# Weighing the one-hot rows on ScalarE instead of VectorE in a graph layer kernel

## The chip, the cores and the metric

The kernel runs on one core of one Trainium2 chip. The metric is the device time of one launch in microseconds (us); lower is better.

## The reference, cut to what matters

The layer normalizes 6250 node rows of 160 features (a layer norm without weights, then relu), multiplies them by two sets of small matrices, and passes messages over 206,250 edges sorted by destination. The shape of the message step is all that matters here:

```python
h = relu(edge_attr_10 @ W_fc1 / sqrt(10)) * sqrt(2)
w = h @ W_fc2 / sqrt(100)                 # (E, 192) -> w0 (64), w1 (64), w2 (32), w3 (32)
y0, y1 = l0[edge_src], l1[edge_src]       # gathered node rows: 64, and 32 x 3
e0, e1 = edge_attr_4[:, :1], edge_attr_4[:, 1:4]
m0 = w0 * y0 * e0
m1 = (w1 * y0)[:, :, None] * e1[:, None, :]
m2 = (w2 * e0)[:, :, None] * y1
m3 = w3 * einsum('eud,ed->eu', y1, e1) / sqrt(3)
s0..s3 = segment_sum(m0..m3, edge_dst)    # per node, / sqrt(16)
out = x + self_part + 0.5 * (s0..s3 by the W_l2 matrices) / sqrt(96)
```

Every message is a product of edge weights and gathered rows, times one of the four attributes of its edge (or, for m3, with the attributes already in the dot product).

## The kernel before, in words

**Node stage (the first 67 us).** The node rows are loaded, normalized, multiplied and written to a table in DRAM. Rows for four edge groups (7, 12, 17 and 22) are computed apart and stay in SBUF (`ahead`), so those groups need no gather.

**Edge stage.** Edges come in tiles of 128 (one per partition) and groups of four tiles (T = 4): 403 groups. Groups go in turns of four (G = 4, slots `j` of the gathered rows `y`), turns in pairs of eight groups. Everything else is double-buffered by the parity `s` of the group. For each group g:

- GpSimd (`gather_group`, L427) issues four indirect DMAs, one a tile, that gather the rows of the sources into `y[:, j]`. It waits for `msg_done` of group g - 4, the last reader of that slot.
- TensorE computes the hidden layer (`fc1`, L976) into `ps_h`; ScalarE applies the relu (`relu`, L547); TensorE computes the 192 weights of each edge (`fc2`, L983) into `ps_w`.
- VectorE (`messages`) writes into slot 0 of `hot[:, s, t]` the one-hot rows: for each edge 32 columns, with a one at its destination's place in a window of 32 nodes (`which`, L746). It then multiplies the vectors of the gathered rows by three attributes (`edge_dots`, L722), writes slots 1 to 4 of `hot`, which are slot 0 times each of the four attributes (`weigh`, L752, one instruction over 128 x 512), sums the dots (`sum_dots`, L727), and forms the messages in three products (L733, L738, L743).
- TensorE (`windows`, L1028 and L1030) multiplies the messages with the weighed one-hot rows: a segment sum of the group into a window of 32 nodes, in `ps_s`. VectorE (`accumulate`, four adds, L815) adds that window to the sums `acc` in SBUF.

**The order of the work is written out by hand**, one instruction stream for each engine, with semaphores. TensorE's step g is `fc1(g)`, `fc2(g - 1)`, `windows(g - 2)`. VectorE's step g is `messages(g)`, `accumulate(g - 1)`. ScalarE's step g is `relu(g)` alone. From the fourth pair on, each pair of eight groups also finishes one block of 128 nodes: ScalarE normalizes it again (`normalize`, L496) at step 1, TensorE turns it (`turn_block`, L989 and L990) before `windows` of step 2, ScalarE copies the turned block (`move_block`, L552) at step 2 and the sums (`copy_block`, L556) at step 3; TensorE waits for that moved block (`hidt_done`) ahead of `fc1` of step 3, and multiplies (`last_linear`, L995 to L1001) at step 7; VectorE adds (`finish`, L800).

SyncE's queue loads the hidden inputs (L275), the indices (L282) and the attributes (L286) by half turns; the attributes wait for `msg_done` of the groups that read the slot before.

**The end.** After the last group's `fc2`, TensorE turns the last two blocks (each needs `normalize` from ScalarE, and both use `turn_block`), and only then runs `windows` of the last group but one, the blocks' own products (L1007, L1008), the sums' products of the last block but one (L1016 to L1018), the last group's windows (`last_windows`, L1040 and L1042), and the last block's products. VectorE's last steps are `last_messages` (the last group in two halves), and two times `accumulate` and `finish`.

Of the kernel before, what the change touches and what calls it, by code (L numbers as in the profile page):

```python
# [76 lines left out]
def gnn_layer(nc, x, x_a, src, dst, radial, attr, avec, w_lin, w_lin_z, w_self, w_self_z, w_last, wf1, wf2, out):  # L77
    ctx = ExitStack()
    with ctx:
# [116 lines left out]
        fc2_done = sem("fc2_done")  # L196
        hot_done = sem("hot_done")
        dots_done = sem("dots_done")
        dot_done = sem("dot_done")
# [58 lines left out]
        def _(sp):  # L258
# [11 lines left out]
            def load_half(i, c, first):  # L270
                k = i * 2 + c
                if not first:
                    sp.wait_ge(fc1_done, (k - 1) * HALF)
                    sp.sem_inc(sp_passed, 1)
                sp.dma_start(rad[:, c, :], radial[:, bass.ds(k * HALF * GE, HALF * GE)]).then_inc(ld_rad[c], 16)  # L275
                if not first:
                    for j in range(HALF * c, HALF * c + HALF):
                        landed = landed_of(i, j)
                        if not isinstance(landed, int) or landed > 0:
                            sp.wait_ge(gathered[j], landed * (16 * T))  # L280
                    sp.sem_inc(sp_passed, 1)
                sp.dma_start(idx[:, c, :], src[:, bass.ds(k * HALF * T, HALF * T)]).then_inc(ld_idx[c], 16)  # L282
                if not first:
                    sp.wait_ge(msg_done, (k - 1) * HALF * 4)
                    sp.sem_inc(sp_passed, 1)
                sp.dma_start(attr_sb[:, c, :, :], attr[:, bass.ds(k * HALF * T, HALF * T), :]).then_inc(ld_attr[c], 16)  # L286
# [87 lines left out]
        def _(pool):  # L374
# [44 lines left out]
            def gather_group(i, j, first, landed):  # L419
                if j % HALF == 0 or (isinstance(i, int) and i * G + j - 1 in AHEAD_GROUPS):  # L420
                    pool.wait_ge(ld_idx[j // HALF], i * 16 + 16)
                if not first:
                    pool.wait_ge(msg_done, (i * G + j - G + 1) * 4)
                    pool.sem_inc(pool_passed, 1)
# [48 lines left out]
        def _(act):  # L473
# [69 lines left out]
            def relu(g, s, first):  # L543
# [3 lines left out]
                nc.scalar.activation(hr[:, s, :], ps_h[0:N_RADIAL, s, 0:GE], ACT.Relu, scale=K_RADIAL).then_inc(relu_done, 1)  # L547

            def move_block(b, n, bank):

# [7 lines left out]
            def windowed():  # L558
                def pair(k, first, finish):
                    for j in range(2 * G):  # L560
                        relu(k * (2 * G) + j, j % 2, first and j < 2)
                        if finish and j == 1:
                            normalize(k - LAG, 0)
# [11 lines left out]
                for j in range(LEFT):  # L575
                    relu((TURNS - 1) * G + j, j % 2, False)
                for n, b in enumerate(range(IN_LOOP, BLOCKS)):
                    normalize(b, n)
# [26 lines left out]
        def _(dve):  # L605
# [143 lines left out]

            def weigh(g, j, s):  # L750
                dve.wait_ge(hot_done, g + 1)
                nc.vector.tensor_tensor(hot[:, s, :, 1:V, :], hot[:, s, :, 0:1, :].to_broadcast([P, T, 4, W]),  # L752
                                        attr_of(j, 0, 4).unsqueeze(3).to_broadcast([P, T, 4, W]), ALU.mult).then_inc(msg_done, 1)

            def messages(i, j):
# [9 lines left out]
                else:  # L765
                    rows = y[:, j, :, :]
                    dve.wait_ge(gathered[j], landed_of(i, j) * (16 * T) + 16 * T)
                    edge_dots(j, rows)
                weigh(g, j, s)
                dve.wait_ge(dots_done, g + 1)  # L770
# [7 lines left out]
            def last_messages():  # L778
# [4 lines left out]
                which(g, s)  # L783
                weigh(g, j, s)
                dve.wait_ge(fc2_done, g + 1)
# [120 lines left out]
        def _(pe):  # L906
# [113 lines left out]
            def windows(g, s, first, block=None):  # L1020

                pe.wait_ge(msg_done, g * 4 + 4)
                if not first:
# [9 lines left out]
            def last_windows():  # L1033

                g, s = EDGE_GROUPS - 1, (EDGE_GROUPS - 1) % 2
                pe.wait_ge(acc_done, (g - 1) * 4)
                for h in range(2):
                    pe.wait_ge(msg_done, g * 4 + 4 + 3 * h)
                    for t in range(h * (T // 2), (h + 1) * (T // 2)):
# [140 lines left out]
```

## Time and profile before

| What | Value |
| --- | --- |
| Time, median of 3 runs | 2081.51 us (2079.91 to 2085.27) |
| The profiled execution | 2082.13 us |
| its span | 2080.4 us |
| its mean granted clock of TensorE | 0.984 |
| TensorE busy (matmul) | 1961.0 us, 94% |
| VectorE busy | 1685.6 us, 81% |
| GpSimd busy | 1570.0 us, 75% |
| ScalarE busy | 352.4 us, 17% |

The times of the trace are microseconds from the start of the span; the span leaves out some 1.7 us of the execution's time. Busy shares are averages over the whole span. A row of the timeline gives the start, the duration, the engine, the line and what it writes and reads, and in brackets how long the engine had been idle and what released it. "x8" is eight instructions in one row. A matmul in fp32 leaves two records. A row of stretches gives the stretch, its length, the busy time of TensorE's matmuls and weight loads, VectorE, ScalarE and GpSimd with their counts, the granted clock, the share of the DMA engines and GB/s.

### The profile page before, as it was taken

The numbers are of one execution on the slowest core, as the hardware profiler recorded it, in microseconds if no ns is written. First come the engines' busy times: TensorE is split into PE (matmuls) and PEld (weight loads), VectorE is DVE, ScalarE is ACT, GpSimd is POOL, SyncE is SP. The second block draws the span as 40 slices with busy tenths as digits, with TensorE's granted clock in tenths as the row PEclk, the third lists the DMA queues.
The fourth block names the chain that finished last, engine by engine and source line by source line (L and its number), as shares of the span: only waits on it lengthen the run. The fifth ranks groups of instructions, "written<-read, shape, count | busy, mean of one in ns | idle before, by whom it ended". The sixth has DMA issues, their size and how long they took to land.

```text
span 2080.4 us, 42104 instructions
## 1 busy us (share of the span) xinstructions
PE 1961.0 (94%) x11562; PEld 1518.1 (73%) x11562; DVE 1685.6 (81%) x4682; ACT 352.4 (17%) x662; POOL 1570.0 (75%) x1639
## 2 busy tenths in 40 slices
PE   6999999999999999999999999999999999999998
PEld 6877777777777777777777777777777777777777
DVE  7799788888888888888888878888788888888887
ACT  6311111111111111111111111111111111111111
POOL 7877777777777777777777777777777777777775
PEclk9999999999999999999999989999999999999999
DMA  6322333333333333333333333333333323333322
GB/s 188 80 68 71 74 72 75 73 73 75 73 73 75 73 72 74 74 74 74 74 74 72 73 74 73 73 75 73 73 75 72 74 72 76 73 74 74 74 72 63
DMA packets 161200, 158.34 MB, mean 76 GB/s; under 512 B 88146, under 2 KB 133110, under 8 KB 161178
## 3 DMA queue, kind: packets, MB, share of 16 engines
q0 software_dynamic: 77376, 132.17, 25.8%
q1 hardware_dynamic: 82088, 24.49, 5.3%
q10 hardware_dynamic: 1714, 1.43, 0.2%
q8 instruction: 8, 0.13, 0.0%
q14 instruction: 14, 0.11, 0.0%
HBM read 149.92 MB, written 8.03 MB: 76 GB/s over the span
## 4 chain that ended last, share of the span: by engine, by line
POOL 36%; issue 26%; DMA 16%; DVE 14%; PE 7%; POOLq 1%; DVEq 0%; ACT 0%; ACTq 0%; SPq 0%
POOL y L427 36%; DMA y<-table,idx 15%; DVE hot L752 4%; DVE msg L733 4%; DVE dot L727 3%; PE ps_w L983 2%; PE ps_s L1028 1%; PE ps_h L976 1%; PE ps_s L1030 1%; DMA xres<-in_x 1%; DVE dots L722 1%; PE ps_w L938 0%; POOLq L438 0%; DVE acc L815 0%; DVEq L818 0%
## 5 line engine op out<-in xcount | busy, mean ns | idle before, releaser
L427 POOL DMA_INDIRECT y<-table,idx x1596 | 1520.6, 953 | 486.4 <-issue 444.8
L983 PEld LDWEIGHTS ps_w<-w_fc,hr 100*128 100x128 f32 x3224 | 516.3, 190 | 316.6 <-issue 316.6
L983 PE MATMUL ps_w<-w_fc,hr 100*128 100x192 f32 x3224 | 635.8, 341 | 0.0
L1028 PE MATMUL ps_s<-hot,msg 128*128 128x128 f32 x3216 | 458.0, 286 | 75.7 <-DVE msg L743 73.2
L547 ACT ACTIVATE hr<-ps_h 100x512 f32<-100x512 f32 x403 | 240.7, 597 | 1640.7 <-PE ps_h L976 1640.7
L1028 PEld LDWEIGHTS ps_s<-hot,msg 128*128 128x128 f32 x3216 | 404.5, 194 | 134.9 <-DVE msg L743 134.5
L722 DVE TENSOR_TENSOR dots<-y,attr_sb 128x384 f32<-128x384 f32 (+1 forms) x400 | 222.8, 557 | 284.9 <-DMA y<-table,idx 284.7
L976 PE MATMUL ps_h<-rad,w_fc 10*100 10x512 f32 x806 | 445.4, 632 | 0.2 <-issue 0.2
L1030 PE MATMUL ps_s<-hot,msg 128*128 128x128 f32 x3216 | 432.5, 278 | 0.0
L1030 PEld LDWEIGHTS ps_s<-hot,msg 128*128 128x128 f32 x3216 | 399.2, 195 | 0.0
L815 DVE TENSOR_TENSOR acc<-acc,ps_s 64x32 f32 (+1 forms) x1612 | 325.3, 202 | 44.5 <-PE ps_s L1030 4.1
L733 DVE TENSOR_TENSOR msg<-ps_w,y 128x512 f32<-128x512 f32 (+1 forms) x400 | 276.0, 690 | 17.4 <-PE ps_w L983 5.0
L752 DVE TENSOR_TENSOR hot<-hot,attr_sb 128x512 f32<-128x512 f32 x403 | 275.9, 685 | 0.0
L727 DVE TENSOR_REDUCE dot<-dots 128x128 f32<-128x384 f32 x404 | 236.2, 585 | 0.0
L738 DVE TENSOR_TENSOR msg<-ps_w,y 128x384 f32<-128x384 f32 (+1 forms) x400 | 218.5, 546 | 0.0
L976 PEld LDWEIGHTS ps_h<-rad,w_fc 10*100 10x100 f32 x806 | 100.2, 161 | 50.3 <-issue 3.1
L746 DVE TENSOR_TENSOR hot<-iota_w,dst_rel 128x128 f32<-128x128 f32 x403 | 117.9, 293 | 14.0 <-issue 1.1
L743 DVE TENSOR_TENSOR msg<-ps_w,dot 128x128 f32<-128x128 f32 x404 | 113.1, 280 | 0.0
L496 ACT ACTIVATE hid<-xres,shift,rstd 128x160 f32 (+1 forms) x98 | 47.9, 510 | 7.1 <-DVE shift L632 7.1
L995 PE MATMUL ps_s<-w_out,fin_in 128*128 128x160 f32 x94 | 25.4, 354 | 21.0 <-DVE msg L743 21.0
L995 PEld LDWEIGHTS ps_s<-w_out,fin_in 128*128 128x128 f32 x94 | 14.5, 191 | 33.2 <-issue 33.2
L556 ACT ACTIVATE fin_in<-acc 128x512 f32 (+1 forms) x49 | 30.5, 622 | 6.3 <-DVE acc L815 6.3
(95 smaller groups left out, 539.3 us busy)
## 6 DMA issues: line engine op xcount, KB each, us to landing
y<-table,idx POOLq DMA_INDIRECT x1596, 2.6
rad<-in_radial SPq DMA_DIRECT2D x202, 40.0 KB
xres<-in_x SPq DMA_DIRECT2D x7, 560.0 KB, 5.3
out<-xres SPq DMA_DIRECT2D x49, 80.0 KB, 1.6
table<-y SPq DMA_DIRECT2D x6, 560.0 KB, 3.7
idx<-in_src SPq DMA_DIRECT2D x202, 4.0 KB
attr_sb<-in_attr SPq DMA_DIRECT2D x202, 16.0 KB
dst_i<-in_dst ACTq DMA_DIRECT2D x1, 808.0 KB, 7.3
```

The costliest lines, as they stand in the source:

```text
L427: nc.gpsimd.indirect_dma_start(out=y[:, j, t, :], out_offset=None, in_=table, in_offset=bass.IndirectOffsetOnAxis(ap=idx[:, j // HALF, col ...
L547: nc.scalar.activation(hr[:, s, :], ps_h[0:N_RADIAL, s, 0:GE], ACT.Relu, scale=K_RADIAL).then_inc(relu_done, 1)
L722: nc.vector.tensor_tensor(dots[:, lo:hi, :, :], vectors(rows, lo, hi), attr_of(j, 1, 4, lo, hi).unsqueeze(3).to_broadcast([P, hi - lo, 3, ...
L727: nc.vector.tensor_reduce(dot[:, lo:hi, :], dots[:, lo:hi, :, :].rearrange("p t d u -> p t u d"), AX.X, ALU.add).then_inc(dot_done, 1)
L733: nc.vector.tensor_tensor(msg[:, s, lo:hi, 0:2 * MUL0].rearrange("p t (k u) -> p t k u", k=2), ps_w[:, s, lo:hi, 0:2 * MUL0].rearrange("p ...
L738: nc.vector.tensor_tensor(msg[:, s, lo:hi, 2 * MUL0:M - MUL1].rearrange("p t (d u) -> p t d u", d=3), ps_w[:, s, lo:hi, 2 * MUL0:NW - MUL1 ...
L752: nc.vector.tensor_tensor(hot[:, s, :, 1:V, :], hot[:, s, :, 0:1, :].to_broadcast([P, T, 4, W]), attr_of(j, 0, 4).unsqueeze(3).to_broadcas ...
L815: nc.vector.tensor_tensor(to, to, p[rows, cols].rearrange("p (v n) -> p v n", n=W), ALU.add).then_inc(acc_done, 1)
L976: nc.tensor.matmul(ps_h[0:N_RADIAL, j % 2, 0:GE], w_fc1[:, :], rad[:, j // HALF, (j % HALF) * GE:(j % HALF + 1) * GE], start=True, stop=Tr ...
L983: ins = nc.tensor.matmul(ps_w[:, s, t, 0:NW], hr[:, s, t * P:(t + 1) * P], w_fc2[:, :], start=True, stop=True)
L1028: nc.tensor.matmul(ps_s[:, s, 0:4 * W], msg[:, s, t, 0:P], hot[:, s, t, 1:V, :], start=(t == 0), stop=(t == T - 1))
L1030: ins = nc.tensor.matmul(ps_s[:, s, 4 * W:8 * W], msg[:, s, t, P:M], hot[:, s, t, 0:4, :], start=(t == 0), stop=(t == T - 1))
```

## The change

VectorE's `weigh` is taken out. ScalarE gets a `weigh` of its own: for each of four tiles and each of four attributes one activation (`Copy`, with the attribute of the partition's edge as its scale operand) over 32 columns, sixteen in a group. It follows `relu` of the next group in ScalarE's stream. A new semaphore, `weighed`, counts groups; `msg_done` counts three for each group instead of four. TensorE's `windows` waits for both, and so does SyncE's load of the attributes; GpSimd's gathers wait for `msg_done` alone.

```diff
@@ SyncE, load_half
                 if not first:
-                    sp.wait_ge(msg_done, (k - 1) * HALF * 4)
+                    sp.wait_ge(msg_done, (k - 1) * HALF * 3)
+                    sp.wait_ge(weighed, (k - 1) * HALF)
                     sp.sem_inc(sp_passed, 1)
@@ GpSimd, gather_group
-                    pool.wait_ge(msg_done, (i * G + j - G + 1) * 4)
+                    pool.wait_ge(msg_done, (i * G + j - G + 1) * 3)
@@ ScalarE
+            def weigh(g, j, s):
+
+                act.wait_ge(hot_done, g + 1)
+                for t in range(T):
+                    for k in range(4):
+                        ins = nc.scalar.activation(hot[:, s, t, 1 + k, :], hot[:, s, t, 0, :], ACT.Copy,
+                                                   scale=attr_sb[:, j // HALF, (j % HALF) * T + t, k:k + 1])
+                ins.then_inc(weighed, 1)
@@ ScalarE, windowed
                     for j in range(2 * G):
                         relu(k * (2 * G) + j, j % 2, first and j < 2)
+                        if j >= 1 or not first:
+                            weigh(k * (2 * G) + j - 1, (j - 1) % G, (j - 1) % 2)
                         if finish and j == 1:
                             normalize(k - LAG, 0)
...
                 for j in range(LEFT):
                     relu((TURNS - 1) * G + j, j % 2, False)
+                    weigh((TURNS - 1) * G + j - 1, (j - 1) % G, (j - 1) % 2)
+                weigh(EDGE_GROUPS - 1, LEFT - 1, (LEFT - 1) % 2)
                 for n, b in enumerate(range(IN_LOOP, BLOCKS)):
                     normalize(b, n)
                     move_block(b, n, n)
@@ VectorE
-            def weigh(g, j, s):
-                dve.wait_ge(hot_done, g + 1)
-                nc.vector.tensor_tensor(hot[:, s, :, 1:V, :], hot[:, s, :, 0:1, :].to_broadcast([P, T, 4, W]),
-                                        attr_of(j, 0, 4).unsqueeze(3).to_broadcast([P, T, 4, W]), ALU.mult).then_inc(msg_done, 1)
@@ VectorE, messages
                     edge_dots(j, rows)
-                weigh(g, j, s)
                 dve.wait_ge(dots_done, g + 1)
@@ VectorE, last_messages
                 which(g, s)
-                weigh(g, j, s)
                 dve.wait_ge(fc2_done, g + 1)
@@ TensorE, windows
-                pe.wait_ge(msg_done, g * 4 + 4)
+                pe.wait_ge(msg_done, g * 3 + 3)
+                pe.wait_ge(weighed, g + 1)
@@ TensorE, last_windows
                 pe.wait_ge(acc_done, (g - 1) * 4)
+                pe.wait_ge(weighed, g + 1)
                 for h in range(2):
-                    pe.wait_ge(msg_done, g * 4 + 4 + 3 * h)
+                    pe.wait_ge(msg_done, g * 3 + 3 + 3 * h)
```

## Rows read from the trace of the kernel before

**Rows 1.** Groups by line and shape: busy us, mean ns, idle before, releasers.
```profile
L427 POOL DMA_INDIRECT y<-table,idx x1596 | 1520.6, 953 | 486.4 <-issue 444.8 <-DVE msg L733 37.3 <-DMA idx<-in_src 2.7
...
L752 DVE TENSOR_TENSOR hot<-hot,attr_sb 128x512 f32<-128x512 f32 x403 | 275.9, 685 | 0.0
...
L547 ACT ACTIVATE hr<-ps_h 100x512 f32<-100x512 f32 x403 | 240.7, 597 | 1640.7 <-PE ps_h L976 1640.7
...
L722 DVE TENSOR_TENSOR dots<-y,attr_sb 128x384 f32<-128x384 f32 x398 | 222.1, 558 | 284.9 <-DMA y<-table,idx 284.7
```

**Rows 2.** Timeline in the middle of the edge stage, one group of VectorE.
```profile
1001.61 0.56 DVE L722 TENSOR_TENSOR dots<-y,attr_sb 128x384 f32<-128x384 f32 x1 [0.85 <-DMA y<-table,idx]
...
1002.08 0.68 DVE L752 TENSOR_TENSOR hot<-hot,attr_sb 128x512 f32<-128x512 f32 x1
...
1002.68 0.59 DVE L727 TENSOR_REDUCE dot<-dots 128x128 f32<-128x384 f32 x1
...
1005.17 0.94 POOL L427 DMA_INDIRECT y<-table,idx  x1 [0.30 <-issue]
...
1005.51 0.29 DVE L746 TENSOR_TENSOR hot<-iota_w,dst_rel 128x128 f32<-128x128 f32 x1
```

**Rows 3.** Timeline, TensorE alone, early in the edge stage: `fc1` of two groups running.
```profile
84.09 1.10 PE L976 MATMUL ps_h<-rad,w_fc 10*100 10x512 f32 x2
...
88.40 1.10 PE L976 MATMUL ps_h<-rad,w_fc 10*100 10x512 f32 x2
```

**Rows 4.** Timeline, ScalarE alone, node stage: activations back to back.
```profile
12.23 0.29 ACT L491 ACTIVATE std<-mean_var,eps 128x7 f32<-128x7 f32 x1
12.43 0.92 ACT L496 ACTIVATE hid<-xres,shift,rstd 128x160 f32 x2
```

**Rows 5.** Timeline at three gathers that took longer, each with VectorE's instruction ahead.
```profile
81.14 0.55 DVE L722 TENSOR_TENSOR dots<-y,attr_sb 128x384 f32<-128x384 f32 x1
81.22 1.29 POOL L427 DMA_INDIRECT y<-table,idx  x1 [0.30 <-issue]
...
98.17 0.29 DVE L746 TENSOR_TENSOR hot<-iota_w,dst_rel 128x128 f32<-128x128 f32 x1
...
98.29 1.00 POOL L427 DMA_INDIRECT y<-table,idx  x1 [0.30 <-issue]
...
2020.18 0.68 DVE L752 TENSOR_TENSOR hot<-hot,attr_sb 128x512 f32<-128x512 f32 x1
2020.34 1.35 POOL L427 DMA_INDIRECT y<-table,idx  x1 [0.30 <-issue]
```

**Rows 6.** Timeline of the end, from the last group but one on.
```profile
2064.74 0.56 DVE L722 TENSOR_TENSOR dots<-y,attr_sb 128x384 f32<-128x384 f32 x1 [0.83 <-DMA y<-table,idx]
...
2066.01 0.28 PE L989 MATMUL ps_h<-ident,hid 128*128 128x128 f32 x1
...
2066.44 0.38 ACT L552 ACTIVATE hid_t<-ps_h 128x256 f32<-128x256 f32 x1 [4.49 <-PE ps_h L990]
...
2066.72 0.51 ACT L496 ACTIVATE hid<-xres,shift,rstd 128x160 f32<-128x160 f32 x1
...
2067.08 0.94 POOL L427 DMA_INDIRECT y<-table,idx  x1 [0.30 <-issue]
2067.28 0.14 PEld L989 LDWEIGHTS ps_h<-ident,hid 128*128 128x128 f32 x1 [1.11 <-ACT hid L496]
...
2067.85 1.16 PE L1028 MATMUL ps_s<-hot,msg 128*128 128x128 f32 x8
...
2073.16 0.39 PE L1042 MATMUL ps_s<-hot,msg 128*128 128x128 f32 x2
...
2074.06 0.91 DVE L815 TENSOR_TENSOR acc<-acc,ps_s 64x32 f32 x4
```

**Rows 7.** TensorE at its lower clock: a timeline row, and a stretch of the end.
```profile
76.96 1.92 PE L1028 MATMUL ps_s<-hot,msg 128*128 128x128 f32 x8
...
2076.00:2078.00 2.00, 1.87 (x8) 1.46 (x7) 0.10 (x1) 0.00 (x0) 0.00 (x0) 0.50 0.00 0
```

More of the change, by code:

```diff
@@ L197, in gnn_layer @@
         hot_done = sem("hot_done")
+        weighed = sem("weighed")
         dots_done = sem("dots_done")
```

## The prediction

> **What bounds the kernel now.** I read the groups by line first. GpSimd's gathers are 1520.6 us busy and 486.4 us between one another [rows 1]: 2007 us of the span of 2080.4. The two parts add to 1.2575 us a gather, and what the group names as idle time is nearly all "issue", the fixed step between two gathers; the 37.3 us "<-DVE msg" are 122 waits of the same 0.3 us, so nothing was waited for. In the timeline GpSimd never pauses from its first gather to the last at 2067.08 [rows 6]. So the time is: a start of some 61 us, 1596 gathers, and a tail of 13 us. A group of four gathers takes 5.01 us.
>
> Next, how near the others are. VectorE is busy 81%, but each group it waits for the gathered rows: 284.9 us in 398 groups, 0.72 each [rows 1]. TensorE looks full at 94%, yet early on, while it works off a backlog, one `fc1` follows the other after 88.40 - 84.09 = 4.31 us [rows 3]. That is its own pace, 0.70 us under GpSimd's. ScalarE is nearly idle [rows 1]. An edit that relieves VectorE therefore gives nothing in the middle unless it reaches the gathers; what it may change is the gathers' length, the tail, and whether ScalarE becomes late.
>
> **Part 1, VectorE loses `weigh`.** 403 x 0.685 = 276 us of busy time go [rows 1]. In the timeline [rows 2] call D the start of the dots (1001.61): `weigh` starts at D + 0.47, the sum at D + 1.07, the next group's `which` at D + 3.90. Without `weigh` the sum must wait for the dots to be written: D + 0.56 and some 0.03, so it comes 0.48 earlier, and with it all that follows: `which` at D + 3.42. The next dots still wait for their gather. Worth in the middle: nothing; VectorE only idles 0.48 more in each group.
>
> **Part 2, the gathers get shorter in places.** A gather takes 0.95, but 35 of them took longer, by 9.0 us together; 26 lie before 211 us. Each had begun just behind a VectorE instruction with two inputs in SBUF: after `dots`, `which` or `weigh` [rows 5]. In all of them the same remainder fits: the gather is held until 0.43 us after `dots` began (81.22 - 81.14 + 1.29 - 0.95 = 0.42), 0.17 after `which` (98.29 - 98.17 + 0.05), 0.56 after `weigh` (0.16 + 0.40). On the gathers' chain every such hold is lost time. Early on VectorE is ahead or behind at TensorE's pace and meets the gathers at changing phases; those until 211 us cost 6.7. Afterwards, with only `dots` and `which`, a meeting at random costs (0.43^2 + 0.17^2)/2/1.25 = 0.085 us a group; 30 groups make 2.5. Gain 4.2 us. In the steady part I take nothing: a gather starts at D + 3.56 [rows 2] and `which` holds it until 3.42 + 0.17 = 3.59, a touch of 0 to 0.03 in some groups (the gap moves by 0.1 with the landing), while the 2.3 us of holds in the rest may shrink. Bounds: a gain of 9.0 (no holds left) and a loss of 6 (0.015 in 400 groups). I take a gain of 4.
>
> This agrees with the Trainium skill, SBUF — State Buffer, the reading of its port diagram: VectorE with two SBUF inputs and GpSimd reading SBUF lock one port pair against each other, ScalarE has its own. By that rule too, the moved work cannot hold a gather any more.
>
> **Part 3, sixteen activations.** The trace has none of 128x32 with one pointer operand. Nearest below: the 128x7 one with a pointer as bias, behind which the next starts 0.20 later (12.43 - 12.23); nearest above: 128x160 with two pointers, 0.92 - 0.51 = 0.41 from one to the next [rows 4]. I take 0.22, by the row with one operand and 25 columns more, and 0.31 for the last of a run. `weigh` is then 15 x 0.22 + 0.31 = 3.6 us. With the relu (0.5 of its 0.60 not overlapped), the block's three activations spread over eight groups (0.2) and a wait (0.05), ScalarE needs 4.35 of 5.01 us a group. It becomes the bound only above (5.01 - 0.75)/16 = 0.27 us a piece.
>
> The Trainium skill (ScalarE: Activation LUTs, What ACT_TABLE_LOAD costs) gives 186 ns plus 93 for a pointer plus 0.833 a column, and 93 of overlap: an estimate of 0.21 a piece. The same page's rules for kernel authors say to multiply on VectorE, not ScalarE. The rows bear it out in the price, 3.6 us against 0.685; what it costs here depends on where ScalarE is waited for.
>
> Is it waited for in the middle? `which` of group g + 1 ends at D + 3.7, its `weigh` runs until D + 7.3; the messages of that group are ready at D + 5.01 + 2.6 = D + 7.6, when TensorE wants `windows`. Behind it `relu` of g + 3 comes at D + 7.9, and TensorE asks for its result more than 2 us later. Just in time, and VectorE reads the window only a group later, 2.5 us of cover more. Cost 0; if a piece takes 0.27, `windows` comes 0.5 late and the cover takes it.
>
> SyncE: the attribute load waits for `weighed` beside `msg_done`, which come within 0.4 us of each other, and the index load queued behind it has 6 us until its gather. GpSimd waits for no new semaphore. Cost 0.
>
> **Part 4, the block step, once in eight groups.** TensorE holds `fc1` of step 3 until `move_block`, now behind `weigh` of step 2's group. `weigh` ends at D + 7.3, the move (0.38 [rows 6]) at D + 7.65, while `windows` of the block's first group ends near D + 5.1: TensorE stands 2.5 us, and 0.7 before `turn_block`. Its spare time in eight groups is 8 x 0.70 less 1.9 for the block's products, 3.7 us. So it is late by 3, and caught up by the next block. VectorE notices lateness over 2.5 us only slightly, and GpSimd only over 10 us, since the gather of g + 6 starts at D + 23.6 for a slot read until D + 12.6. Cost 0 to the end. What this stretch can do is drop TensorE's clock: a like idle time of 2 us near the end left 0.50 granted [rows 7].
>
> **Part 5, the tail.** Now D is 2064.74, the dots of the last group but one [rows 6]. `which` of the last group ends at D + 3.71 and ScalarE is free; its `weigh` ends 3.6 later. Only then come the last blocks: by the spacings of the rows, `normalize` to turn 0.56, turn to move 0.43, move to the second `normalize` 0.28, again 0.56, and 0.57 to `windows` of the last group but one. That is D + 3.71 + 0.05 + 3.6 - 0.1 + 2.4 = D + 9.66, or 2074.4; before, 2067.85. TensorE then has the same unbroken run until its last window product (2073.16 + 0.39 = 2073.55). VectorE's last sums began 0.5 behind it (2074.06) and will now follow at once: +6.1. TensorE has been idle for over 6 us, so this run begins at the lower clock, where eight products take 1.92 instead of 1.06 to 1.16 [rows 7]. Its 5.7 us would grow by up to 4.6; I take half, 2.3, and nothing for the products after it, which were slow before. Tail +8.4, bounds +5 (clock up, last products fast) and +11.
>
> **Sum.** 2082.13 (the profiled execution: span 2080.4 and 1.7 around it) - 4 + 8.4 = 2086.5; the median of the runs lies 0.6 lower, so 2086.0. That is +0.2%: inside the 0.3%, 6.2 us, that a measurement of this kernel can tell from no change, and not by much.
>
> **The rivals.**
> - *A long tail with no gain at the gathers: slower.* Place: from 2067 on, ScalarE's last `weigh` ahead of `normalize`. Price: 6.1 for the order and 4.6 for the low clock, the gathers held as before. 2081.5 + 10.7 = 2092. It decides from the point where tail less gathers' gain passes 6.2, that is when the whole run stays at the low clock, or the gathers gain under 2. For it: the idle time is sure. Against: the clock rose within 10 us at the start. Chance 0.30.
> - *ScalarE is the bound.* At the middle of the two rows, 0.305 a piece, a group takes 16 x 0.305 + 0.75 = 5.63; 403 groups and 69 + 17 us around them make about 2355. It needs over 0.27, against the row with one operand. Chance 0.07.
> - *The block step paces.* TensorE's stand of 3 us plus low clock behind it passes the 3.7 us it has. Each us over is 47 us in 47 blocks: 2095 to 2130. Against: when TensorE is late, `weigh` is already done and the stand shrinks to 1. Chance 0.06.
> - *Faster.* All 9 us of holds go and the tail hides ScalarE's work, leaving nothing: 2073. The order of the tail speaks against it. Chance 0.04.
> - Forecast: 0.53.
>
> So faster 0.04, same 0.53, slower 0.43. The range takes in the tail's and the gathers' bounds and the first rival: 2080.5 to 2095.5.
>
> **What would show it.** Right: GpSimd's gathers still without a pause, their mean a few ns lower; `Copy` rows 0.21 to 0.22 apart, ScalarE near 85% busy; VectorE's wait for gathers near 1.2 us a group; a pause of TensorE of some 2.5 us once in 40 us; at the end `windows` of the last group but one 9.7 us behind the last full dots, released by ScalarE. Wrong: gathers waiting for messages or indices, `which` holding the first gather of each group, or ScalarE without idle time.

## The result, and the profile after

| | before | changed |
|---|---|---|
| median | 2083.39 us (7 runs, 2079.91 to 2089.38) | 2089.68 us (7 runs, 2086.55 to 2091.87) |
| ratio to before | | 1.0030, 95% interval 1.0019 to 1.0042 |
| profiled execution | 2082.13, span 2080.4 | 2089.65, span 2087.9 |
| mean granted clock of TensorE | 0.984 | 0.960 |

The change costs 6.3 us, 0.3%. That lies on the line between "same" and "slower" as the prediction drew it, and inside its range.

The page of the changed kernel, its first part: VectorE has lost 199 us of busy time (`weigh` was 276 us of instructions, but they overlapped their neighbours), ScalarE has gained 1369 (352 before), TensorE and GpSimd are as they were.

```profile
PE 1955.0 (94%) x11562; PEld 1563.1 (75%) x11562; DVE 1486.4 (71%) x4279; ACT 1721.4 (82%) x7110; POOL 1568.2 (75%) x1639
```

The groups by line and shape, to be read against [rows 1]:

```profile
L429 POOL DMA_INDIRECT y<-table,idx x1596 | 1518.7, 952 | 488.0 <-issue 435.3 <-DVE msg L753 43.9 <-DMA idx<-in_src 4.2
L556 ACT ACTIVATE hot<-hot,attr_sb 128x32 f32<-128x32 f32 x6448 | 1408.5, 308 | 126.1 <-DVE hot L761 114.7 <-issue 11.0
...
L984 PE MATMUL ps_h<-rad,w_fc 10*100 10x512 f32 x806 | 451.0, 639 | 93.6 <-ACT hid_t L563 93.4 <-issue 0.2
...
L737 DVE TENSOR_TENSOR dots<-y,attr_sb 128x384 f32<-128x384 f32 x398 | 222.0, 558 | 355.0 <-DMA y<-table,idx 353.9
```

Three things are to be seen. The gathers plus what lies between them are 1518.7 + 488.0 = 2006.7, where before they were 2007.0: the chain that sets the middle has hardly moved. VectorE, relieved of `weigh`, spends 69 us more waiting for the same gathers (353.9 against 284.7). And `fc1` has a new wait for ScalarE's `move_block`, 93.4 us. That wait is 47 waits of about 2 us, one in each block, as the list of waits says (count, then longest):

```profile
PE ps_h L984 <- ACT hid_t L563: 93.4, 47, 2.7
```

One of the 47, in the timeline of the middle:

```profile
1019.30 0.94 POOL L429 DMA_INDIRECT y<-table,idx  x1 [0.30 <-issue]
1019.35 3.50 ACT L556 ACTIVATE hot<-hot,attr_sb 128x32 f32<-128x32 f32 x16 [0.62 <-DVE hot L761]
...
1019.59 1.06 PE L1039 MATMUL ps_s<-hot,msg 128*128 128x128 f32 x8
...
1022.76 0.36 ACT L563 ACTIVATE hid_t<-ps_h 128x256 f32<-128x256 f32 x1
...
1023.17 1.10 PE L984 MATMUL ps_h<-rad,w_fc 10*100 10x512 f32 x2 [2.53 <-ACT hid_t L563]
...
1026.31 1.92 PE L1037 MATMUL ps_s<-hot,msg 128*128 128x128 f32 x8
...
1028.07 0.94 POOL L429 DMA_INDIRECT y<-table,idx  x1 [0.30 <-issue]
```

`weigh` is one unbroken block of 3.50 us, sixteen pieces; `move_block` stands behind it, TensorE stands for 2.53 us. Then `windows` needs 1.92 us, the price of the lower clock [rows 7], until 1028. GpSimd goes on through all of it: the row at 1028.07 is the seventh gather behind the one at 1019.30, one every 1.25 us. The clock shows the same in the mean: its lower level is half speed (0.50 granted [rows 7]), so 0.984 is (1 - 0.984)/0.5 x 2080 = 67 us at it, 0.960 is 167 us. So TensorE is at the lower level for about 100 us more than before, and but for the few us at the end none of it reaches the time, because TensorE isn't the bound.

Where the 6.3 us are is seen in the timeline of the end, to be read against [rows 6]:

```profile
2064.51 0.56 DVE L737 TENSOR_TENSOR dots<-y,attr_sb 128x384 f32<-128x384 f32 x1 [1.42 <-DMA y<-table,idx]
...
2066.82 0.94 POOL L429 DMA_INDIRECT y<-table,idx  x1 [0.30 <-issue]
...
2068.26 3.50 ACT L556 ACTIVATE hot<-hot,attr_sb 128x32 f32<-128x32 f32 x16 [1.63 <-DVE hot L761]
...
2071.66 0.51 ACT L498 ACTIVATE hid<-xres,shift,rstd 128x160 f32<-128x160 f32 x1
...
2072.22 0.47 PE L997 MATMUL ps_h<-ident,hid 128*128 128x128 f32 x1 [6.37 <-ACT hid L498]
...
2074.27 1.91 PE L1037 MATMUL ps_s<-hot,msg 128*128 128x128 f32 x8
...
2081.99 0.39 PE L1052 MATMUL ps_s<-hot,msg 128*128 128x128 f32 x2
2082.52 0.91 DVE L823 TENSOR_TENSOR acc<-acc,ps_s 64x32 f32 x4 [1.50 <-PE ps_s L1052]
...
2085.39 0.38 DVE L808 SCALAR_TENSOR_TENSOR xres<-ps_h,a_sb,xres 128x160 f32<-128x160 f32 x1 [1.96 <-PE ps_h L1026]
```

The last gather starts 0.26 us earlier than before. From there to the end of VectorE's last instruction it takes 2085.39 + 0.38 - 2066.82 = 18.95 us. Before it took 2077.90 + 0.38 - 2067.08 = 11.20, with this row as the last of VectorE's:

```profile
2077.90 0.38 DVE L800 SCALAR_TENSOR_TENSOR xres<-ps_h,a_sb,xres 128x160 f32<-128x160 f32 x1 [2.94 <-PE ps_h L1018]
```

That is 7.75 more, and the span is 7.5 longer. TensorE stands for 6.37 us, and what releases it is `normalize`, which is queued on ScalarE behind the last `weigh`. Behind this stand the products run at the lower level; the very last ones are on the upper level again, as this stretch shows (1.00 granted):

```profile
2084.00:2086.00 2.00, 1.21 (x8) 0.97 (x8) 0.38 (x1) 0.09 (x1) 0.00 (x0) 1.00 0.00 0
```

### The profile page after: what moved, and what is told of

Same layout as the page of the kernel before. It is cut to its first block, busy times and chain, and to the rows that moved or that the text cites. A ratio compares the mean times of both kernels' runs of the same rounds, so it can differ in the third digit from the quotient of the medians.

```text
span 2087.9 us, 48635 instructions
## 1 busy us (share of the span) xinstructions
PE 1955.0 (94%) x11562; PEld 1563.1 (75%) x11562; DVE 1486.4 (71%) x4279; ACT 1721.4 (82%) x7110; POOL 1568.2 (75%) x1639
## 4 chain that ended last, share of the span: by engine, by line
PE 25%; POOL 19%; DMA 17%; issue 16%; DVE 15%; ACT 4%; DVEq 3%; POOLq 0%; ACTq 0%; SPq 0%
POOL y L429 19%; DMA y<-table,idx 17%; PE ps_w L991 8%; PE ps_h L984 5%; PE ps_s L1037 5%; PE ps_s L1039 4%; DVE dot L742 4%; DVE dots L737 4%; ACT hot L556 3%; DVEq L826 3%; DVE msg L753 3%; DVE msg L748 1%; DVE acc L823 1%; DMA xres<-in_x 1%; PE ps_w L946 0%
## 5 line engine op out<-in xcount | busy, mean ns | idle before, releaser
L429 POOL DMA_INDIRECT y<-table,idx x1596 | 1518.7, 952 | 488.0 <-issue 435.3
L556 ACT ACTIVATE hot<-hot,attr_sb 128x32 f32<-128x32 f32 x6448 | 1408.5, 308 | 126.1 <-DVE hot L761 114.7
L991 PEld LDWEIGHTS ps_w<-w_fc,hr 100*128 100x128 f32 x3224 | 535.4, 196 | 322.1 <-issue 322.1
L991 PE MATMUL ps_w<-w_fc,hr 100*128 100x192 f32 x3224 | 660.3, 350 | 0.0
L984 PE MATMUL ps_h<-rad,w_fc 10*100 10x512 f32 x806 | 451.0, 639 | 93.6 <-ACT hid_t L563 93.4
L1037 PEld LDWEIGHTS ps_s<-hot,msg 128*128 128x128 f32 x3216 | 433.8, 202 | 2.7 <-DVE acc L823 0.4
L1039 PEld LDWEIGHTS ps_s<-hot,msg 128*128 128x128 f32 x3216 | 405.5, 198 | 0.0
L924 PE MATMUL ps_h<-ident,hid 128*128 128x128 f32 x49 | 14.9, 322 | 16.9 <-ACT hid L498 16.6
L808 DVE SCALAR_TENSOR_TENSOR xres<-ps_s,a_sb,xres 128x160 f32 x47 | 17.7, 378 | 17.8 <-PE ps_s L1039 17.8
```

What stands on the lines that cost most here:

```text
L429: nc.gpsimd.indirect_dma_start(out=y[:, j, t, :], out_offset=None, in_=table, in_offset=bass.IndirectOffsetOnAxis(ap=idx[:, j // HALF, col ...
L556: ins = nc.scalar.activation(hot[:, s, t, 1 + k, :], hot[:, s, t, 0, :], ACT.Copy, scale=attr_sb[:, j // HALF, (j % HALF) * T + t, k:k + 1])
L984: nc.tensor.matmul(ps_h[0:N_RADIAL, j % 2, 0:GE], w_fc1[:, :], rad[:, j // HALF, (j % HALF) * GE:(j % HALF + 1) * GE], start=True, stop=Tr ...
L991: ins = nc.tensor.matmul(ps_w[:, s, t, 0:NW], hr[:, s, t * P:(t + 1) * P], w_fc2[:, :], start=True, stop=True)
L1037: nc.tensor.matmul(ps_s[:, s, 0:4 * W], msg[:, s, t, 0:P], hot[:, s, t, 1:V, :], start=(t == 0), stop=(t == T - 1))
L1039: ins = nc.tensor.matmul(ps_s[:, s, 4 * W:8 * W], msg[:, s, t, P:M], hot[:, s, t, 0:4, :], start=(t == 0), stop=(t == T - 1))
```

## The experiments

The change leaves two suspects with a place (the order of ScalarE's work in the block step and at the end), one with a size (how long VectorE holds the gathers) and the question what the weighing costs at all. All kernels are edits of the changed one.

Three of the four sets ran on chips on which the kernel before itself takes 2942, 2841 or 2838 us and not 2083. So each ratio below is to the runs of the kernel before on the same chip, with its 95% interval in brackets.

### Order at the end, order in the block step, both, and no weighing

`tail_order`, in ScalarE's last turn:

```
                     relu((TURNS - 1) * G + j, j % 2, False)
+                    if j == LEFT - 1:
+                        for n, b in enumerate(range(IN_LOOP, BLOCKS)):
+                            normalize(b, n)
                     weigh((TURNS - 1) * G + j - 1, (j - 1) % G, (j - 1) % 2)
-                weigh(EDGE_GROUPS - 1, LEFT - 1, (LEFT - 1) % 2)
                 for n, b in enumerate(range(IN_LOOP, BLOCKS)):
-                    normalize(b, n)
                     move_block(b, n, n)
+                weigh(EDGE_GROUPS - 1, LEFT - 1, (LEFT - 1) % 2)
```

> The changed kernel with one edit, at the end of ScalarE's stream: both last blocks are normalized behind the last relu and moved ahead of the last group's weighing. Theory (the loss is the order of the tail): TensorE's windows of the last group but one start near 2068 instead of 2074.3, so it does not fall to the lower clock; 6 to 8 us less than the changed kernel, 2081 to 2084. Rival (the loss lies in the middle, by waits of TensorE or ScalarE): less than 2 us gained.

`block_order`, in ScalarE's loop over pairs of turns:

```
                         relu(k * (2 * G) + j, j % 2, first and j < 2)
-                        if j >= 1 or not first:
-                            weigh(k * (2 * G) + j - 1, (j - 1) % G, (j - 1) % 2)
                         if finish and j == 1:
                             normalize(k - LAG, 0)
                         if finish and j == 2:
                             move_block(k - LAG, 0, 1)
+                        if j >= 1 or not first:
+                            weigh(k * (2 * G) + j - 1, (j - 1) % G, (j - 1) % 2)
```

> The changed kernel with one edit in the loop: normalize and move_block come ahead of weigh in ScalarE's stream. Theory (TensorE's stand of 2.5 us once in eight groups is covered, for the gathers never wait): TensorE's wait for the moved block, 93 us in all, goes to under 10, the mean granted clock rises from 0.96 to 0.98 or more, and the time stays within 2 us of the changed kernel, 2088 to 2091. Rival (the stand and the low clock behind it pace the loop or disturb the gathers): 3 us or more gained.

`both_orders` has both edits.

> Both edits together. Theory: as the tail edit alone, 2081 to 2084, within 1 us of it. Rival (the block step costs): 3 us or more below the tail edit alone.

`unweighed` takes ScalarE's weighing away but for two groups, and TensorE and SyncE wait for those two alone:

```
-                        if j >= 1 or not first:
+                        if first and 1 <= j < 3:
                             weigh(k * (2 * G) + j - 1, (j - 1) % G, (j - 1) % 2)
...
-                    weigh((TURNS - 1) * G + j - 1, (j - 1) % G, (j - 1) % 2)
-                weigh(EDGE_GROUPS - 1, LEFT - 1, (LEFT - 1) % 2)
```

> The changed kernel without weighing, but for the first two groups: slots 1 to 4 of the one-hot rows keep their first content, so the segment sums are not the reference's. Neither VectorE nor ScalarE does the work. Theory (the gathers are the bound, and only the tail and their holds count): the last gather starts within 4 us of the one before, the end follows it as in the kernel before or up to 1 us sooner: 2077 to 2083. Rival (taking the work off VectorE is worth time by itself, and ScalarE's lateness eats it): under 2072.

They ran together on a first chip (before: 2941.75 us) and again on a second (before: 2841.09 us). The expectations of the second time:

> The tail edit once more, on another chip, for the first took place where the kernel before takes 2942 us. Theory (the loss is the order of the tail): 6 to 8 us less than the changed kernel, so 0.9985 to 1.0005 of the kernel before; TensorE's windows of the last group but one near 2068. Rival (the loss lies in the middle): 1.002 or more.

> The block edit once more, on another chip. Theory: TensorE's wait for the moved block goes to under 10 us in all and the clock rises, but the time stays that of the changed kernel, 1.002 to 1.004 of the kernel before. Rival (the stand and the low clock pace the loop): 1.0015 or less.

> Both edits once more. Theory: within 0.0005 of the tail edit alone, 0.9985 to 1.0005. Rival (the block step costs where the gathers pace): 0.997 or less.

> Nothing weighed but the first two groups, once more; the segment sums are not the reference's. Theory (the gathers are the bound): 0.997 to 1.0005 of the kernel before. Rival (relief of VectorE is worth time by itself): under 0.995.

| kernel | ratio, first chip (before 2941.75) | ratio, second chip (before 2841.09) | wait of `fc1` for `move_block`, second chip |
|---|---|---|---|
| tail_order | 1.0185 (1.0123 to 1.0246) | 1.0378 (1.0325 to 1.0432) | 148.5 us |
| block_order | 1.0104 (1.0065 to 1.0142) | 1.0274 (1.0222 to 1.0325) | 66.0 us |
| both_orders | 1.0082 (1.0049 to 1.0115) | 1.0249 (1.0201 to 1.0296) | 87.2 us |
| unweighed | 0.9883 (0.9835 to 0.9932) | 1.0030 (0.9995 to 1.0066) | 25.3 us |

The expected times and ratios were worked out for chips with the times of the first comparison, and none of them came; `both_orders` is under `tail_order` on both chips, which its rival had said. One expected wait doesn't hang on those times: `block_order` was to bring the wait of `fc1` for `move_block` under 10 us, and it came out at 105.8 us on the first chip and 66.0 on the second. With both edits it was 99.9 and 87.2, and with no weighing at all still 30.1 and 25.3.

Where the two chips lose their time shows in the list of waits of the second `tail_order`:

```profile
POOL y L429 <- DVE msg L760: 647.3, 171, 9.1
...
POOL y L429 <- issue: 492.4, 1371, 6.6
```

GpSimd, which on the chip of the first comparison waited for nobody, now waits 647 us for messages to be done with its slots. The messages hang on TensorE's results, and its weight loads and products come with gaps in which it waits for nothing that the profile shows, as in this timeline (of `two_inputs`, below; a like chip):

```profile
1022.96 0.41 PEld L1040 LDWEIGHTS ps_s<-hot,msg 128*128 128x128 f32 x3 [1.22 <-issue]
...
1025.06 0.29 PEld L1040 LDWEIGHTS ps_s<-hot,msg 128*128 128x128 f32 x1 [1.69 <-issue]
1025.06 0.58 PE L1040 MATMUL ps_s<-hot,msg 128*128 128x128 f32 x1 [1.07 <-issue]
```

The mean granted clock is 0.80 there. So I read TensorE as the bound on these chips, and the same kernels answer another question: what does ScalarE's weighing cost when nothing covers TensorE's lateness? Weighed on ScalarE, the kernels take 1 to 4% more than the kernel before. Without the weighing the time is that of before, or a per cent under it; `both_orders` is 2.0 and 2.2% above that, `tail_order` 3.0 and 3.5%. From `tail_order` to `both_orders`, which differ by the block step's order alone, the ratio falls by 1.0 and 1.3%, some 30 and 37 us for 47 blocks; on the second chip `fc1` waits 61 us less for `move_block`. The edit at the end moves the time much less: from `block_order` to `both_orders` the ratio falls by 0.2 and 0.25%, 6 and 7 us, inside the intervals. The stand of TensorE in the block step that the first comparison shows as free (93.4 us, 47 waits) is paid for here.

What the end's edit gives can't be read from these ratios, but the timelines allow it. From the last full dots to `windows` of the last group but one it is 4.67 and 4.77 us in the two traces of `tail_order` and 5.03 and 4.67 in those of `both_orders`, against 10.44 and 10.20 in `block_order`, which has the changed kernel's end, where it was 9.76. So the order of ScalarE's work at the end makes 5 to 6 us of TensorE's lateness there, with or without the block step's edit. The stretch from the last gather to the end scatters more, but agrees: on the second chip it is 19.95 us in `tail_order`, 35.5 in `block_order`, 26.1 in `both_orders`, 21.1 in `unweighed`; on the first 25.6, 37.1, 28.8 and 24.9. The timeline of the second `tail_order` shows what the edit leaves:

```profile
2911.91 3.49 ACT L556 ACTIVATE hot<-hot,attr_sb 128x32 f32<-128x32 f32 x16
2915.30 0.62 ACT L567 ACTIVATE fin_in<-acc 128x512 f32<-128x512 f32 x1
...
2915.98 0.63 PE L1026 MATMUL ps_h<-w_out,fin_in 128*128 128x32 f32 x4 [1.56 <-ACT fin_in L567]
```

The last `weigh` now delays the copy of the sums, and TensorE waits for that instead. So wherever it stands, the last weighing is in something's way. That led to the next kernel.

### The last group weighed by VectorE again

`end_by_vector` has the block step's order, normalizes the last two blocks one group earlier than `tail_order`, and gives VectorE the weighing of the last group back, at the instruction's old price of 0.69 us [rows 1], in place of ScalarE's 3.5:

```
                     relu((TURNS - 1) * G + j, j % 2, False)
+                    if j == LEFT - 2:
+                        for n, b in enumerate(range(IN_LOOP, BLOCKS)):
+                            normalize(b, n)
                     weigh((TURNS - 1) * G + j - 1, (j - 1) % G, (j - 1) % 2)
-                weigh(EDGE_GROUPS - 1, LEFT - 1, (LEFT - 1) % 2)
                 for n, b in enumerate(range(IN_LOOP, BLOCKS)):
-                    normalize(b, n)
                     move_block(b, n, n)
@@ VectorE, last_messages
                 which(g, s)
+                dve.wait_ge(hot_done, g + 1)
+                nc.vector.tensor_tensor(hot[:, s, :, 1:V, :], ..., ALU.mult).then_inc(msg_done, 1)
@@ TensorE, last_windows
-                pe.wait_ge(weighed, g + 1)
-                    pe.wait_ge(msg_done, g * 3 + 3 + 3 * h)
+                    pe.wait_ge(msg_done, g * 3 + 4 + 3 * h)
```

> The block edit of block_order, and another end: the last two blocks are normalized behind the last relu but one, moved behind the weighing of the last group but one, and the last group is weighed by VectorE as in the kernel before. Theory (the whole loss lies behind the last gather, by the order of ScalarE's stream and the copy of the sums behind its weighing): from the last gather's start to the end of VectorE's last instruction 10.5 to 11.5 us (11.2 before, 19.0 changed), the last gather within 3 us of the one before, 0.997 to 1.000 of the kernel before. Rival (the middle costs as well): the tail as said, but 1.002 or more of the kernel before.

It ran on a chip with the times of the first comparison (before 2084.32 there): 2079.5 us, ratio 0.9982, interval 0.9970 to 0.9994. That is 0.2% under the kernel before, little but clear of 1, and inside the expected 0.997 to 1.000. The timeline of its end:

```profile
2062.00 0.56 DVE L738 TENSOR_TENSOR dots<-y,attr_sb 128x384 f32<-128x384 f32 x1 [1.27 <-DMA y<-table,idx]
...
2063.18 0.28 PE L1001 MATMUL ps_h<-ident,hid 128*128 128x128 f32 x1
...
2064.35 0.95 POOL L429 DMA_INDIRECT y<-table,idx  x1 [0.30 <-issue]
...
2064.63 1.16 PE L1041 MATMUL ps_s<-hot,msg 128*128 128x128 f32 x8 [0.85 <-DVE msg L759]
...
2065.75 0.69 DVE L795 TENSOR_TENSOR hot<-hot,attr_sb 128x512 f32<-128x512 f32 x1
...
2069.95 0.39 PE L1055 MATMUL ps_s<-hot,msg 128*128 128x128 f32 x2
...
2073.73 0.38 DVE L812 SCALAR_TENSOR_TENSOR xres<-ps_h,a_sb,xres 128x160 f32<-128x160 f32 x1 [1.96 <-PE ps_h L1030]
```

and its stretch with the last products:

```profile
2072.00:2074.00 2.00, 1.21 (x8) 0.97 (x8) 0.27 (x1) 0.43 (x1) 0.00 (x0) 1.00 0.08 25
```

The transpose of the last blocks is done before the last gather has begun; TensorE waits 0.85 us, and for messages. The last gather to the end: 2073.73 + 0.38 - 2064.35 = 9.76 us, against 18.95 changed and 11.20 before; 10.5 to 11.5 had been expected. Against the changed kernel, TensorE isn't late and doesn't fall to the lower level: eight products of `windows` take 1.16 us and not 1.91. Against the kernel before, where they took 1.16 too [rows 6], two things are shorter. `windows` of the last group but one starts 0.28 us behind the last gather's start and not 0.77. And the last block's products run on the upper level (1.00 granted, against 0.50 before [rows 7]), so that from the row of the last window products to VectorE's last row it is 2073.73 - 2069.95 = 3.78 us and not 2077.90 - 2073.16 = 4.74. Why the level fell there in the one and not in the other isn't shown. The ratio fell from 1.0030 to 0.9982, by 10 us, and the tail is 9.2 us shorter in the traces. With the tail mended the loss is gone: that shows its cause. How much of it is the order and how much the price of the last weighing this kernel doesn't separate; the two traces of `tail_order` above show the order alone.

The block step's order came along in the same kernel. It did what it says: `fc1` no longer waits for ScalarE.

```profile
L429 POOL DMA_INDIRECT y<-table,idx x1596 | 1516.1, 950 | 488.0 <-issue 441.2 <-DVE msg L754 38.1 <-DVE msg L759 3.5
...
L988 PE MATMUL ps_h<-rad,w_fc 10*100 10x512 f32 x806 | 446.4, 633 | 0.2 <-issue 0.2
```

But GpSimd's idle time is 488.0 us with the 93.4 us of stands and 488.0 without them, and from 170 us on, ahead of the first block step near 180, no gap between two gathers is over 0.35 us in either trace. So the stands were free here, though the two edits weren't run apart on a chip with these times. Ahead of that GpSimd did stop in this trace, twice, and both times for messages, 0.5 and 0.96 us above the usual 0.30 (the second is put down to "issue", but its wait ends 0.03 us behind the messages):

```profile
137.66 0.28 DVE L759 TENSOR_TENSOR msg<-ps_w,dot 128x128 f32<-128x128 f32 x1
...
138.74 0.94 POOL L429 DMA_INDIRECT y<-table,idx  x1 [0.80 <-DVE msg L759]
...
159.22 0.28 DVE L759 TENSOR_TENSOR msg<-ps_w,dot 128x128 f32<-128x128 f32 x1
...
160.30 0.94 POOL L429 DMA_INDIRECT y<-table,idx  x1 [1.26 <-issue]
```

The last gather starts 2.5 us sooner than in the changed kernel. That comes from nothing the edit does: gathers that nothing held took 945.3 ns in this execution, 948.1 in that of the changed kernel and 947.0 before, and 2.8 ns over 1595 steps are 4.5 us (with the gaps 4.9), of which 1.7 go to more holds and 0.65 to a later first gather.

The other traces tell whether this length belongs to the kernel or to the execution. It has two levels: 944.9 to 945.3 ns in five of the fourteen traces, 947.0 to 948.1 in nine. One and the same kernel shows both: `block_order` 947.8, 947.3 and 945.0 in its three traces, `unweighed` 947.7 and 944.9. And each of the three chips with more than one trace shows both. So the level goes with neither the kernel nor the chip, but with the execution. What sets it isn't shown.

### What holds a gather

The prediction's gain rested on a reading of [rows 5]: VectorE's instruction with two inputs in SBUF holds a gather that begins inside it. Two kernels add one instruction of the same length, ahead of `which`, 403 times. One has two inputs in SBUF, the other a single one; neither result is used. `block_order` ran beside them once more, as the third of the set (the two were put on the changed kernel).

```
@@ VectorE, which; two_inputs
+                nc.vector.tensor_tensor(hid[:, 2:6, 0:P], w_out[:, :, 0:P], ones[:, :].unsqueeze(1).to_broadcast([P, 4, P]), ALU.mult)
@@ VectorE, which; one_input
+                nc.vector.tensor_reduce(hid[:, 2, 0:P], w_out[:, :, 0:P].rearrange("p v (b c) -> p v b c", c=4), AX.X, ALU.add)
```

> The changed kernel with one idle instruction more on VectorE in each group, ahead of which: a product of two SBUF tensors over 128x512, its result unused. It begins 3.4 us behind the dots, just ahead of a gather. Theory (a VectorE instruction with two SBUF inputs holds a gather that begins behind it, for 0.56 us from its own start): gathers longer by 0.2 us a group on the mean, the last gather 50 to 110 us later, 2135 to 2205 us in all. Rival (the long gathers had another cause): VectorE has 0.9 us to spare in a group, so within 5 us of the changed kernel.

> The control: in the same place a reduce over 128x512 with one SBUF input, of about the same length. Theory: it holds no gather; within 5 us of the changed kernel, 2085 to 2095. If the length of VectorE's stream and not the second input lengthens the gathers: as two_inputs.

> The block edit alone, a third time, now where the kernel before takes its 2080 to 2085 us. Theory (with ScalarE's stream as changed at the end, all of the loss stays, for it lies behind the last gather): 1.002 to 1.004 of the kernel before; TensorE's wait for the moved block under 10 us in all; end 18 to 20 us behind the last gather. Rival (the block step was part of the loss): 1.0015 or less, with the end still 18 us or more behind the last gather.

Measured, with the kernel before at 2838.03: `two_inputs` 1.0349 (1.026 to 1.0438), `one_input` 1.0286 (1.0206 to 1.0367), `block_order` 1.0240 (1.0181 to 1.0299). TensorE was the bound once more, so the times say nothing on the holds, and none of the expected times can be judged: a held gather has slack here. Of `block_order`'s other signs neither came: `fc1` waited 82.4 us for the moved block, and the end was 29.3 us behind the last gather. The gathers' own rows do say it. Groups of `two_inputs`:

```profile
L429 POOL DMA_INDIRECT y<-table,idx x1596 | 1571.1, 984 | 1254.2 <-DVE msg L758 601.5 <-issue 477.0 <-DMA idx<-in_src 144.7
...
L761 DVE TENSOR_TENSOR hid<-w_out,ones 128x512 f32<-128x512 f32 x403 | 279.2, 693 | 13.3 <-issue 0.8
```

and of `one_input`:

```profile
L429 POOL DMA_INDIRECT y<-table,idx x1596 | 1535.6, 962 | 1287.4 <-DVE msg L758 570.9 <-issue 496.4 <-DMA idx<-in_src 190.8
...
L761 DVE TENSOR_REDUCE hid<-w_out 128x128 f32<-128x512 f32 x403 | 276.4, 686 | 13.2 <-issue 0.8
```

Both instructions take 0.69 us, and the gathers differ by 1571.1 - 1535.6 = 35.5 us. In `two_inputs` 122 gathers began inside the added instruction and were 40.3 us longer together; in `one_input` 102 did, and were 0.01 us longer together. Two pairs from the timeline of `two_inputs`:

```profile
327.08 0.69 DVE L761 TENSOR_TENSOR hid<-w_out,ones 128x512 f32<-128x512 f32 x1
327.15 1.44 POOL L429 DMA_INDIRECT y<-table,idx  x1 [3.97 <-DVE msg L758]
...
615.56 0.69 DVE L761 TENSOR_TENSOR hid<-w_out,ones 128x512 f32<-128x512 f32 x1
615.95 1.12 POOL L429 DMA_INDIRECT y<-table,idx  x1 [0.30 <-issue]
```

and the like of the first from `one_input`:

```profile
329.59 0.69 DVE L761 TENSOR_REDUCE hid<-w_out 128x128 f32<-128x512 f32 x1
329.66 0.94 POOL L429 DMA_INDIRECT y<-table,idx  x1 [3.97 <-DVE msg L758]
```

327.15 + 1.44 - 0.95 - 327.08 = 0.56, and 615.95 + 1.12 - 0.95 - 615.56 = 0.56: the gather is held until 0.56 us after the instruction began, whenever it began itself. Over all 122 it is 0.567. The added reduce is another operation than the added product, so the difference could lie in that. The message products settle it: they are TENSOR_TENSOR like the added one, but with one input in PSUM, and 403 gathers that began inside one in the trace of before were 0.01 us longer together. The prediction's reading stands, and its numbers: 0.17 for `which`, 0.43 for `dots`, 0.56 for 512 columns.

## Why the prediction was right, and where not

**The bound.** Right: GpSimd's gathers run on until the last, but for one pause of 1.5 us near 124 us (below), with TensorE and VectorE late or idle beside them.

**VectorE without `weigh`.** Right that it is worth nothing by itself. Its wait for the gathered rows rose from 0.72 to 353.9/398 = 0.89 us a group, not to the 1.2 named. The rest of what was freed goes into a wait for TensorE that was 4.1 us in all before:

```profile
DVE acc L823 <- PE ps_s L1039: 94.5, 130, 6.7
```

In 130 places TensorE, behind its stand or at the lower clock, is now later than VectorE, and still GpSimd never pauses for it. "VectorE notices lateness over 2.5 us only slightly" was too small for this, though it costs nothing.

**The gathers' gain.** This is the term that was mis-sized: 4 us predicted, 0.3 measured (the last gather starts at 2066.82 and not at 2067.08). The holds did shrink, from 9.0 to 5.4 us, by 3.6, where 4.2 were worked out. The steady part, for which a touch in some groups was named and nothing taken, shows it: 242 gathers began inside `which` and lost 1.9 us together; 26 began inside `dots` and lost 3.4. What ate the gain is not among the holds. Once GpSimd stood for 1.8 us, which the profile puts down to the index load:

```profile
119.50 0.34 SPq L283 DMA_DIRECT2D idx<-in_src  x1
120.12 1.27 POOL L429 DMA_INDIRECT y<-table,idx  x1 [0.30 <-issue]
...
124.44 1.27 POOL L429 DMA_INDIRECT y<-table,idx  x1 [1.79 <-DMA idx<-in_src]
```

That is 1.5 us above the usual 0.30; before, the longest gap lost 0.2, so 1.3 more. But the indices weren't late. SyncE issued their load 4.9 us ahead of the gather, and its packets were in by 122.31; GpSimd's own wait for them and for `msg_done` began only at 123.64 and was over in 0.04 us. So neither the indices nor SyncE's new wait for `weighed` held this gather. GpSimd came late to its wait, 1.0 us behind the end of the gather ahead (122.65), and the cause of that is open. It is the only such stand: 9 are put down to the index load, and the other eight are of 0.3 us. And each undisturbed gather with the gap behind it took 1.2 ns longer, 1595 x 1.2 = 1.9 us; since one kernel shows steps up to 2.8 ns apart in different executions, this needs no effect of the change, and nothing shows one. -3.6 + 1.3 + 1.9 + 0.1 of a later start gives -0.3. The step of the prediction that was off is that the sum counted the holds alone and took the length of all other gathers, and of the gaps, as fixed.

**The activations.** Right in price and in effect: sixteen take 3.50, so (3.50 - 0.31)/15 = 0.213 a piece, 0.22 taken. ScalarE is busy 82% and never paces the gathers. This agrees with the estimate of 0.21 from the Trainium skill (ScalarE: Activation LUTs, What ACT_TABLE_LOAD costs). The same page's rule (Rules for kernel authors) to multiply on VectorE is borne out in the one place where ScalarE's lateness reaches the end: with the last group weighed by VectorE again, and `normalize` ahead, the kernel is 10 us faster. For the other groups the rule changes nothing here; on the chips where TensorE is the bound, the kernel before, which does as the rule says, is 1 to 4% faster.

**The block step.** Right: a stand of 2.5 us (2.53 in the one shown, 93.4/47 = 1.99 on the mean), the lower clock behind it, nothing to the end. Its weight depends on the bound, which the prediction's rival "the block step paces" named and two other chips showed.

**The tail.** Right. `windows` of the last group but one was put at 9.66 us behind the last full dots and came at 2074.27 - 2064.51 = 9.76. VectorE's last sums were put 8.4 us later and came 2082.52 - 2074.06 = 8.46 later, or 8.72 counted from the last gather. Behind them the last products ran at the upper level, which they hadn't before; that gave 0.97 back and makes the tail 7.75 longer in all. "Nothing for the products after it, which were slow before" was a little too dear.

**The sum.** From profiled execution to profiled execution +4.4 was forecast and +7.5 measured: 3.7 of the gathers' gain are missing, and the tail is 0.65 cheaper. The medians differ by 6.3, less than that, because the median of before with seven runs is 1.3 above its profiled execution and that of the changed kernel is at its own. So the tail's +8.4 was right and the gathers' -4 was not, which moves the result towards the first rival. That rival's own path, the gathers held as before and all of TensorE's run at the lower clock, is not what happened either: its tail was 10.7. That "same" came out and not the rival's "slower" is in part luck: the measured 0.30% lies on the line that the prediction drew, and of the two terms that made up its sum one did not come.

## What to carry to other kernels

Work that moves to an idle engine at five times the price is free as long as a queue of other work hides it; look at the two places where that queue is empty, the last group and any step whose order on that engine puts the long work ahead of something short that another engine waits for. Give the last instance back to the fast engine, or put the short work first. And a gain that is a sum of many small holds should be set against how much the base step moves from one execution to the next: 1 ns in 1596 gathers is 1.6 us, and the step moved by up to 2.8 ns.

## What the runs showed of the hardware

A VectorE instruction with two fp32 inputs in SBUF holds a GpSimd gather that begins inside it until 0.17 (128 columns), 0.43 (384) or 0.56 us (512) after the instruction's start, which is 0.12 us before its recorded end (0.29, 0.55, 0.69). One with a single input of the same 0.69 us held nothing, 0.01 us in 102 gathers, and neither did products with one input in PSUM. The Trainium skill (SBUF — State Buffer, Terms) says that the port pair is held for the full instruction; the trace agrees in that an instruction with two SBUF inputs holds the gather and those with one do not, but the hold ends before the record does.

A gather of 128 rows that nothing held, and that waited for nothing, took 944.9 to 945.3 ns in five executions and 947.0 to 948.1 in nine, whatever the kernel; over 1596 gathers that is up to 5 us.

Three of the chips ran the kernel before in 2838 to 2942 us and not in 2083, with TensorE's mean granted clock near 0.80. In the traces taken there TensorE stands for up to 3.0 us (`two_inputs`) or 7.5 (the first `unweighed`) ahead of the weight loads of `fc2` with no wait to show for it, against 1.6 in the traces of the first comparison. There I read TensorE and not GpSimd as the bound, and kernels of this change, which stand between -0.2 and +0.3% on the other chips, cost up to 3.8%. What causes it isn't shown by the traces.
